# Graph attention and mixture of experts on one core: bf16 parts of the projected rows in place of float32 copies, and the comparisons moved to VectorE

## What is computed

```python
h = (layernorm(x) @ W.T).reshape(n, 8, 32)
alpha = sum(h[src] * a_src) + sum(h[dst] * a_dst)
alpha = alpha + sum(relu(edge_attr @ edge_W.T + edge_b) * h[dst])   # per edge and head
alpha = leaky(alpha, 0.2)
attn = softmax of alpha over the edges of each target
x = x + segment_sum(h[src] * attn, dst) + bias
x = x + top-2 of 8 experts (256 -> 1024 -> gelu -> 256) of layernorm(x), weighted
```

## Time and profile before

| what | us |
|---|---|
| median of three runs | 2126.27 |
| the profiled execution, its own time | 2128.02 |
| its span, from the first to the last instruction | 2126.0 |
| end of `prepare` (start of the first instruction of `edges`) | 81.3 |
| first instruction of `aggregate` | 128.1 |
| last `expand` begins | 1176.3 |
| first gather of rows by GpSimd | 84.0 |
| first work of `attend` | 1211.1 |
| first work of `experts` | 1346.3 |

### The profile page before, as it was taken

How to read it: one execution, slowest core, us unless ns; L and a number is a source line. 1 busy time by engine, 2 the same in 40 slices (tenths; PEclk the granted TensorE clock), 3 DMA queues, 4 the chain that set the end, 5 groups by cost and what they waited for, 6 DMA issues and landing times. The chain is left out here.

```text
span 2126.0 us, 41064 instructions
## 1 busy us (share of the span) xinstructions
PE 2009.7 (95%) x11612; PEld 1585.9 (75%) x11612; DVE 1515.8 (71%) x3458; ACT 1352.4 (64%) x3892; POOL 1181.9 (56%) x1125
## 2 busy tenths in 40 slices
PE   7799999999999999999999676899999999999997
PEld 6566666766666666666666434899999999999996
DVE  7289999999999999999999897544444444444442
ACT  4698888988988988988988565433333333333332
POOL 1377777776776766666666000355555555555553
PEclk9899999999999999999999887999999999999998
DMA  9766565555555555555554688222222222222221
GB/s 252 227 194 175 170 186 175 172 179 165 169 176 163 167 170 163 158 168 160 157 165 143 230 267 190 46 39 36 38 39 36 38 38 36 38 38 36 38 38 23
DMA packets 160559, 270.94 MB, mean 127 GB/s; under 512 B 36239, under 2 KB 114864, under 8 KB 160211
## 3 DMA queue, kind: packets, MB, share of 16 engines
q0 software_dynamic: 61920, 139.45, 27.6%
q1 hardware_dynamic: 89706, 121.22, 18.6%
q10 hardware_dynamic: 8712, 7.65, 1.1%
HBM read 231.06 MB, written 37.17 MB: 126 GB/s over the span
## 5 line engine op out<-in xcount | busy, mean ns | idle before, releaser
L679 POOL DMA_INDIRECT arena<-h_tab,src x784 | 759.6, 969 | 375.6 <-issue 211.8
L1687 ACT ACTIVATE arena<-psum,arena 128x128 f32<-128x128 f32 x840 | 240.1, 368 | 518.2 <-PE psum L1637 518.2
L881 PE MATMUL psum<-arena 128*128 128x256 f32 x1760 | 479.1, 395 | 9.9 <-DVE arena L973 8.0
L902 PE MATMUL psum<-arena 128*128 128x264 f32 x1760 | 475.0, 393 | 2.5 <-DVE arena L996 2.4
L1637 PEld LDWEIGHTS psum<-arena 128*128 128x128 f32 x3360 | 392.9, 192 | 7.5 <-issue 2.2
L902 PEld LDWEIGHTS psum<-arena 128*128 128x128 f32 x1760 | 320.4, 190 | 100.3 <-issue 50.8
L1637 PE MATMUL psum<-arena 128*128 128x128 f32 x3360 | 393.4, 276 | 1.8 <-DVE arena L1709 1.8
L881 PEld LDWEIGHTS psum<-arena 128*128 128x128 f32 x1760 | 318.8, 191 | 98.2 <-issue 42.5
L1653 PE MATMUL psum<-arena 128*128 x1680 | 379.8, 379 | 0.0
L1599 POOL DMA_INDIRECT out_rows<-arena,src x105 | 208.3, 1984 | 247.2 <-DVE arena L1722 244.2
L1653 PEld LDWEIGHTS psum<-arena 128*128 128x128 f32 x1680 | 311.1, 190 | 38.0
(11 more groups left out here) (233 smaller groups left out, 1917.9 us busy)
## 6 DMA issues: line engine op xcount, KB each, us to landing
arena<-rel_list SPq DMA_DIRECT2D x110, 512.0 KB
arena<-in_W SPq DMA_DIRECT2D x16, 1024.0 KB, 12.3
arena<-h_tab,src POOLq DMA_INDIRECT x784
arena<-ea_slots SPq DMA_DIRECT2D x440, 27.0 KB
arena<-in_x SPq DMA_DIRECT2D x12, 896.0 KB, 8.5
h_tab<-arena SPq DMA_DIRECT2D x6, 952.0 KB, 7.9
out_rows<-arena SPq DMA_DIRECT2D x5, 896.0 KB, 5.4
xn<-arena ACTq DMA_DIRECT2D x5, 896.0 KB, 6.9
```

Of the source, the lines that this page charges most:

```text
L679: pool.indirect_dma_start(rows[:, (p % RING * U + k) * TW:(p % RING * U + k + 1) * TW], None, d.h_tab[:, :], bass.IndirectOffsetOnAxis(ap= ...
L881: last = nc.tensor.matmul(ps[:, HDT + x, y * UE:(y + 1) * UE], hj[:, (s // 2 * 2 + y) % HJ, x * P:(x + 1) * P], oht[:, half % OT, (u + y) ...
L902: last = nc.tensor.matmul(ps[:, AGG + a % 2, 0:HS], oh[:, a % OH, k, :], msg[:, a % MSG, k, :], start=(k == 0), stop=(k == U - 1))
L1687: last = nc.scalar.activation(hT[:, b, h * P:(h + 1) * P], ps[:, UP + 2 * b + half, h % 4 * P:(h % 4 + 1) * P], ACT.Gelu, bias=b1_now[:, b ...
```

## The change

Each projected row is kept as three bf16 parts whose sum is the float32 value (first: the value cast to bf16; rest: value minus first; second: rest cast; third: rest minus second). They lie for all 49 tiles in SBUF (`parts`, 384 words a tile) in place of `h_all` and the four `hj` buffers.

- `prepare`: three staging buffers of 7 tiles take the projected rows. GpSimd makes the parts of groups 0 to 5, four instructions of 128x1792 elements a group, once the group is copied out; ScalarE waits for the parts and the store of group i-3 before it writes group i. VectorE copies the targets to bf16.
- `edges`: VectorE makes the parts of group 6 in steps 2 to 5. `expand` uses six bf16 matmuls of 256 columns (three parts, two slots) in place of two float32 ones; their weights are read at register addresses, for which TensorE loads 8 words a chunk. `node_rows` and ScalarE's `select` go; VectorE makes all four `oht` pieces, bf16 in place, and the loads L692 are 256 KB. The sums lie over parts of node tiles that are passed; ScalarE clears two tiles (2 x 264 words) at a time, four times a chunk.
- The order of the weights: W1's second halves of five experts at the end of `edges` (5 x 0.5 MB), three of W2 and the rest of W1's second halves and one first half (5 MB) ahead of the first store in `attend`, five more of W2 (5 MB) between its later loads, and seven first halves of W1 in `route` (3.5 MB).

```diff
+def parts_of(c, i):
+    h = c.stage[i % 3].rearrange("p (k h f) -> p k h f", h=H, f=FW)[:, :, :, 1:D + 1]
+    rest = c.arena[:, LISTS:LISTS + REST_WORDS].rearrange("p (k h f) -> p k h f", k=GT, h=H)
+    group = c.arena[:, PARTS_AT + i * GT * ST:PARTS_AT + (i + 1) * GT * ST].bitcast(BF16).rearrange("p (k q h f) -> p k q h f", k=GT, q=PARTS, h=H)
+    return (h, rest, *(group[:, :, q] for q in range(PARTS)))
...
@@ prepare, gpsimd
+            for i in range(GROUPS - 1):
+                h, rest, first, second, third = parts_of(c, i)
+                pool.wait_ge(h_copied, (i + 1) * GT + 2)
+                nc.gpsimd.tensor_copy(first, h).then_inc(cast, 1)
+                pool.wait_ge(cast, 4 * i + 1)
+                nc.gpsimd.tensor_tensor(rest, h, first, ALU.subtract).then_inc(cast, 1)
+                pool.wait_ge(cast, 4 * i + 2)
+                nc.gpsimd.tensor_copy(second, rest).then_inc(cast, 1)
+                pool.wait_ge(cast, 4 * i + 3)
+                nc.gpsimd.tensor_tensor(third, rest, second, ALU.subtract).then_inc(cast, 1)
+                pool.wait_ge(cast, 4 * i + 4)
@@ prepare, scalar, take_h
+                    if i >= 3:
+                        act.wait_ge(rows_stored[i - 3], 32)
+                        act.wait_ge(cast, 4 * (i - 3) + 2)
...
@@ edges, gpsimd
-            pool.wait_ge(c.rows_stored, 16 * (GROUPS + 1))
+            for i in range(GROUPS):
+                pool.wait_ge(c.group_moved[i], 48 if i == GROUPS - 1 else 32)
@@ edges, scalar
-            def clear_sums(k):
...
+            def clear_ahead(j, k):
+                if k == 0:
+                    act.wait_ge(split, 4)
+                two = acc[:, ds((j + 2 * k + 1) * ST, 2 * ST)].rearrange("p (b n) -> p b n", b=2)[:, :, 0:HS]
+                nc.scalar.activation(two, c.ones[:, 0:1].unsqueeze(2).to_broadcast([P, 2, HS]), ACT.Copy, scale=0.0).then_inc(cleared, 1)
...
-            def select(g):
...
-                    node_rows(t + 2, js)
...
-                if t % CS == 3 and by_scalar((t + 3) // 2) and t + 3 < SLOTS:
-                    select((t + 3) // 2)
@@ edges, tensor, expand
-                    pe.wait_ge(hj_made, s + 2)
...
-                    last = nc.tensor.matmul(ps[:, HDT + x, y * UE:(y + 1) * UE], hj[:, (s // 2 * 2 + y) % HJ, x * P:(x + 1) * P],
-                                            oht[:, half % OT, (u + y) * UE:(u + y + 1) * UE], start=True, stop=True)
+                    j = js[(s // 2 * 2 + y) % CS]
+                    for q in range(PARTS):
+                        last = nc.tensor.matmul(ps[:, HDT + x, y * UE:(y + 1) * UE], parts[:, ds(j * (PARTS * IN) + (q * IN + x * P), P)],
+                                                oht[:, half % OT, (u + y) * UE:(u + y + 1) * UE], start=(q == 0), stop=(q == PARTS - 1))
...
+                    if t % CS == CS - 1 and t + 1 < SLOTS:
+                        js = load_words(nc, c.slots[0:1, t + 1:t + 1 + CS], mybir.EngineType.PE, 0, J - 1)
@@ edges, vector
+                if 2 <= t < 6:
+                    part(t - 2)
...
-                if t % CS in AHEAD_OF and SELECTED * 2 <= t + AHEAD_OF[t % CS] < SLOTS and not by_scalar((t + AHEAD_OF[t % CS]) // 2):
+                if t % CS in AHEAD_OF and SELECTED * 2 <= t + AHEAD_OF[t % CS] < SLOTS:
@@ attend, sync
-            for e in range(W2_LATE, X):
+            def second_weights(e):
                 sp.dma_start(c.w2[:, e], d.W2[e].rearrange("(h p) n -> p h n", p=P)).then_inc(c.w2_loaded, 16)
+            for e in range(3):
+                second_weights(e)
+            for e in range(W1_EARLY, X):
+                sp.dma_start(w1[:, 1, e, :], d.W1[e, P:2 * P, :]).then_inc(c.w1_loaded, 16)
+            sp.dma_start(w1[:, 0, X - 1, :], d.W1[X - 1, 0:P, :]).then_inc(c.w1_loaded, 16)
...
+                for e in AFTER_MEAN.get(i, ()):
+                    sp.wait_ge(mean_made, i + 1)
+                    second_weights(e)
```

More of the change, by code:

```diff
@@ L146, in take @@
                 return c.arena[rows, self.at - n:self.at]
-        work, lists = Region(H_AT + J * TW, ACC_AT), Region(ACC_AT, REST_AT)
+        lists, early = Region(0, LISTS), Region(LISTS, REST_AT)
         row = slice(0, 1)
-        h_all = c.h_all
-        x_all = work.take(J * IN)
-        w_nat = work.take(KH * IN).rearrange("p (k i) -> p k i", k=KH)
+        x_all = c.arena[:, X_AT:REST_AT]
+        w_nat = early.take(KH * IN).rearrange("p (k i) -> p k i", k=KH)
+        below = early.take(PAIRS)
+        hi_tile, iota_t, val_row = (early.take(PAIRS, row) for _ in range(3))
+        assert early.at >= LISTS + REST_WORDS
+        work, late = Region(early.at, ACC_AT), Region(ACC_AT, PARTS_AT)
+        two_stages = work.take(2 * GT * TW)
+        c.stage = [late.take(GT * TW), two_stages[:, 0:GT * TW], two_stages[:, GT * TW:]]
         a_bd = work.take(KH * 2 * H).rearrange("p (k h) -> p k h", k=KH)
@@ L163, in prepare @@
         xT = work.take(3 * IN).rearrange("p (b i) -> p b i", b=3)
-        hi_row, hi_tile, iota_t, val_row, last_i = (work.take(PAIRS, row) for _ in range(5))
+        hi_row, last_i = (work.take(PAIRS, row) for _ in range(2))
         p_int, p_by32, p_by8 = (work.take(1) for _ in range(3))
@@ L1065, in _, with part @@
             nc.vector.tensor_scalar(c.ends, c.ends, -0.5, 2 * BIG, ALU.add, ALU.mult).then_inc(ends_listed, 1)
-            dve.wait_ge(cleared, 3)
+            dve.wait_ge(marked, 3)
+            def part(n):
+                h, rest, first, second, third = parts_of(c, GROUPS - 1)
+                if n:
+                    dve.wait_ge(split, n)
+                if n == 0:
+                    last = nc.vector.tensor_copy(first, h)
+                elif n == 1:
+                    last = nc.vector.tensor_tensor(rest, h, first, ALU.subtract)
+                elif n == 2:
+                    last = nc.vector.tensor_copy(second, rest)
+                else:
+                    last = nc.vector.tensor_tensor(third, rest, second, ALU.subtract)
+                last.then_inc(split, 1)
             for t in range(STEPS):
@@ L1134, in attend @@
         LAST = len(TILES)
+        AFTER_MEAN = {1: (3,), 2: (4, 5), 3: (6,), 4: (7,)}
+        assert all(W2_AT + (e + 1) * (HID // P) * IN <= ACC_AT + FIRST[i + 1] * ST for i, es in AFTER_MEAN.items() for e in es)
         bank = lambda n: n % 3
```

199 lines of the change are left out of this document (97 added, 102 removed).

## The result

The changed kernel takes 2147.85 us, the median of 4 runs (2147.57 to 2149.08), against 2126.62 for the kernel before beside it (4 runs, 2123.89 to 2133.44). The ratio is 1.0096, with a 95% interval of 1.0081 to 1.0111: slower by 1.0%, where 2113 us and "faster" had been forecast. The time lies in the upper part of the range that was given, 2080 to 2152, which was there for the rivals with a late start. The profiled execution took 2148.03 us, with a span of 2145.7.

What follows compares the result with a forecast made beforehand. The prediction took TensorE to set the loop's pace, VectorE 0.67 us a chunk behind, GpSimd's gathers level early. Its sum was 2128.0 - 31 (loop) - 3 (filling) + 14 (first stage) + 5 (`attend`) = 2113 us, range 2080 to 2152.

Steps and rivals of the forecast that it cites:

- the rivals with a late start: Slower cases where the gathers start late: behind GpSimd's parts, 2140 us, chance 0.17; or with VectorE gaining nothing.
- 34.1 + 64 = 98: First stage: GpSimd, free at 34.1 us, makes six groups of parts at 10.6 us each, ending at 98 us.
- +14 us: First stage: gathers start at about 98 us in place of 84.0, all of it on the path.
- The rival of the barrier: End of `prepare`: all engines wait for group 5's parts; at 15.2 us a group, +41 us, 2140 us, chance 0.17.
- ScalarE's wait for the parts of group i-3 is met in time: First stage: at 10.6 us a group on GpSimd, ScalarE's wait is met in time.
- VectorE's chunk: Edge loop: bf16 comparisons at 0.26 us and no aggregation wait bring a chunk of 8 slots from 19.87 to 19.07 us.
- The wait of 0.67 goes since TensorE has 1.8 us a chunk less to do: Edge loop: VectorE's wait of 0.67 us a chunk for TensorE's aggregation, behind the long reduction, vanishes.
- The term: Edge loop: 313 slots from slot 127 on gain 0.100 us each, -31 us.
- The filling: Start of the edge loop: rid of the clears and bounded by gathers, 41 us instead of 44, -3 us.
- GpSimd as the floor: Edge loop: gathers at 1.27 us each set the pace, so the new pace is reached only from slot 127.
- `attend`: Weight loads share DMA with stores and loads of x: +5 us, between nothing and 13.
- The signs that were to show the forecast wrong: Chunk above 19.6 or below 18.5 us, gathers over 1.27 apart, bf16 weight-load gaps, first `expand` before 95 or after 125.

Runs made afterwards that it cites:

- before_gp_clean: The kernel before with only GpSimd's 24 instructions for the parts added, their results unused: 2156.73 us, ratio 1.0130.
- msg3_clean: The changed kernel with three message buffers instead of two: 2122.12 us, ratio 0.9968.
- best: best_msg2 with three message buffers instead of two: 2100.58 us, ratio 0.9867 to the kernel before.
- after_same: The changed kernel as it is, run again: 2148.30 us, ratio 1.0091 to the kernel before.
- best_msg2: first_stage with W2's loads moved from `attend` to `route` and each group's first cast moved from VectorE to ScalarE: 2131.66 us, ratio 1.0010.
- first_stage: The changed kernel with GpSimd's parts given to VectorE, in the first stage and the loop's filling: first gather at 98.56 us instead of 116.9; total not used (pauses).

## Why the prediction was wrong

**The first stage is the step that failed.** The step is "34.1 + 64 = 98", and from it "+14 us". The size of a group was right (10.8 us undisturbed against 10.6, and against 11.4 by the figure of the Trainium skill, "GPSIMD Engine Reference", "Elementwise — side-by-side cycle accounting", which the prediction gave); the sum was not. It took the stretch of 49.8 us in which GpSimd waited as free, and asked only for GpSimd's own length. What was late next was VectorE, then ScalarE, TensorE and GpSimd again. +33 us instead of +14; in before_gp_clean, where the clash stands alone, 29 us at the first gather are 28 in the time. The rival of the barrier had the place (all engines wait for the parts; it was to decide from an end at 113 us, and the end was 114.8) and the sign, but its mechanism, 15.2 us a group, isn't what happened. "ScalarE's wait for the parts of group i-3 is met in time" was right; its wait for the store of group 0 (7.2 us), which the stage buffers bring, was not in the sum.

**VectorE's chunk.** Comparison (0.26), `expand` (0.65) and hidden weight loads were right. (`expand`'s matmuls stood 14.5 us between 300 and 1100 us, all of it for VectorE's product, none for a weight load of 98 ns.) "The wait of 0.67 goes since TensorE has 1.8 us a chunk less to do" was wrong: the wait belongs to one place in the chunk, and most of TensorE's saving lies in others. In this one the expansion begins only behind VectorE's product, the reduction and the aggregation behind it, and the message of two steps on needs the buffer that this aggregation frees. msg3_clean shows it: with one more buffer the chunk is 18.93 us, even below the 19.07 forecast.

The term came out at -24 between first aggregation and last `expand` instead of -31, and that it came so near is partly luck. The prediction had no gain in the first 109 slots behind the first aggregation and 31 us in the rest. By the starts of the aggregations the first 109 gained 7 us (265.9 us against 273.0) and the other 312 only 16 (759.6 against 775.9). In msg3_clean it is 8 and 38.

The filling came out at +3 instead of -3. The trace shows a part: two gathers held by VectorE's subtractions (2.6 and 1.8 us) put the 33rd gather 42.7 us behind the first, where it was 41.1. The rest was not taken apart.

**GpSimd as the floor** was right in kind: 80 gathers in 100 us up to 500 us, and in best the chunks are 19.8 us on average from 240 to 360 us and mostly 18.8 to 18.9 after. As a bar to any gain before slot 127 it was too high, by the 7 us above.

**`attend`** was right: +6.8 against +5 (0 to 13), +9.7 in after_same, from the wait that the prediction named.

The terms as they came: +33, +3, -24, +7 and about +1 for the rest, 20 us, where the sum had +14, -3, -31 and +5. The signs that were to show the forecast wrong would not have done so: the chunk (19.46 us) and the first `expand` (124.2 us) both lie just inside them.

## What to carry to other kernels

An engine that idles is not free while it shares something with a busy one: before work goes to GpSimd, list VectorE's operations of that stretch with two SBUF operands or a cast, and allow for the length of GpSimd's instruction with each that can meet one; the other way round, keep long two-operand work of VectorE's away from gathers that are on the path. A wait behind a long instruction of another engine went away here by one more buffer, not by making the other engine faster elsewhere; the buffer gave 26 us here, and the whole rewrite of the expansion gave 24 in the loop. A transfer moved out of a crowded stage is worth only what the next stage doesn't pay for it: here `attend` fell by 3 us or more, and `route` grew by 3.

## What the runs showed of the hardware

- VectorE's instruction stands to the end of GpSimd's: 7 elements in 3.05 us, with two operands in SBUF. GpSimd is held too: its subtraction of 1792 elements is 3.5 us alone and up to 4.4 beside VectorE's.
- VectorE's subtraction of 1792 elements (2.01 us) holds a gather of GpSimd's: the gather ended 0.83 us behind the subtraction, 2.0 to 2.9 us long in place of 0.95 (best_msg2). VectorE's casts of the same size did not hold one.
- Cutting an undisturbed GpSimd subtraction in seven raised it from 3.5 to 4.4 us.
- VectorE's cast of 1792 elements with gaps took 2.01 us, of 1024 without gaps 0.69 (first_stage): 1.12 against 0.67 ns an element.
- The same program can run a sixth slower in the edge loop, with pauses of 1.5 to 6.6 us on VectorE and ScalarE that no event of the trace explains, while the first stage and `attend` keep their lengths. The kernel before took 2476 us at one time and 2129 at another on what is recorded as the same chip, so it isn't shown to be a matter of the chip.
